# Two attentions and a gated MLP on one core: which PSUM banks the turn of maxima and the side products use, and the order in pair 22

## The chip, the cores and the metric

One core of a Trainium2 chip. The metric is the device time of one execution in microseconds. Before the change three timed runs gave 481.25, 480.57 and 481.23, median 481.23 us.

## What is computed

Two transformer blocks on x (2 x 512 x 128) with a context (2 x 154 x 96), all in 32-bit precision. Block 0 is a cross attention with 16 heads of 8 and an MLP. Block 1 is a self attention, a cross attention on the context (both with 16 heads of 64) and a gated MLP, each behind a layernorm. Cut to what matters here:

```python
def _attn(xq, xc, Wq, Wk, Wv, Wo, bo):
    q = (xq @ Wq).reshape(B, N, HEADS, D_HEAD)
    k = (xc @ Wk).reshape(B, S, HEADS, D_HEAD)
    v = (xc @ Wv).reshape(B, S, HEADS, D_HEAD)
    scores = jnp.einsum('bnhd,bshd->bhns', q, k) * scale
    attn = jax.nn.softmax(scores, axis=-1)
    out = jnp.einsum('bhns,bshd->bnhd', attn, v).reshape(B, N, HEADS * D_HEAD)
    return out @ Wo + bo
x = _attn(_ln(x, g1, b1), _ln(x, g1, b1), Wq1, Wk1, Wv1, Wo1, bo1) + x
x = _attn(_ln(x, g2, b2), context, Wq2, Wk2, Wv2, Wo2, bo2) + x
x = _geglu_ff(_ln(x, g3, b3), Wp, bp, Wf, bf) + x
```

## The kernel before

The program is written engine by engine with semaphores; nothing reorders it. The attentions of block 1 are a loop over 32 pairs `g` of heads (two heads of 64 fill 128 partitions): pairs 0 to 15 are the self attention (batch 0, then 1), pairs 16 to 31 the cross attention. A pair's softmax is computed with keys on partitions, so the maxima over keys, one for each query, are needed as a row that is added to the scores in the accumulation.

For pair `g` TensorE does, in `attention` (L925):

- `all_scores(g)` (L874): the scores in chunks of keys (four in a self pair, two in a cross pair). A chunk is three products of rounded and rest parts (L714) and the product that adds the row of maxima (L717). Between them lie the products for the maxima of pair `g + 1`, with queries on partitions (`head_max`, L680).
- `side_before(g)`, then `project(g + 2)` (queries and keys of a later pair; L625, in a cross pair also L669).
- `turn_pair(g + 1)` (L694): four transposes that turn the maxima of the next pair, of 128 queries each, into the row.
- `side_behind(g)`, `denominators` (L749) and `weigh(g, c)` (L734), the product of the exponentials with the values, into PV.

The side steps are other parts of the network that are laid into the loop: values (`VALUES`), the spread of the inverse denominators over the partitions (`spread_inverse`, L776, by the table `SPREADS`), output projections (L787), and the turns of the layernormed features (`turn`, L503). In pair 21 the turn of the second batch's features for the cross attention comes last of all; pair 22 projects with them for pair 24, and pair 30 has the turn for the last layernorm.

PSUM has 8 banks. Four are two bank pairs `ST0` and `ST1`, the ring of scores; two, `M0` and `M1`, serve the maxima; the last two are PV and DEN. `claim` hands out the ring's pairs in turn and waits until the use two claims back is freed; `claim_m` does the same with the single banks M0 and M1:

```python
def claim(key, freed, count):
    k = len(s_uses)
    if k >= 2:
        pe.wait_ge(*s_uses[k - 2])
    s_uses.append((freed, count))
    ring[key] = k % 2
    return ST[k % 2]
```

Chunks of scores (freed by the exponential), projections (freed by VectorE's rest part, `lo`), values, the turn of the maxima (freed by ScalarE's copy of the row, `mrow_set`) and some spreads use the ring. Each maxima product claims one bank M, which VectorE's reduction (L1645, in cross pairs L1647) frees.

ScalarE's order in a pair: the copy of the weighted sum of the pair before out of PV (`weighted`, L1313), the exponentials (L1305), values, the rounded part of the projection (`leading`, L1286 or L1288 and L1289), the row of maxima (`maxima_rows`, L1295). In pair 22 the features come first of all (`scale_features(2, 1)`, L1264 full and L1266 rounded). VectorE's: the reductions of the maxima of pair g + 1, the rest part (`trailing`), and side steps: in pair 22 the rest of the features (`trailing_features`, L1619: full less rounded part). The projection of the first pair of a batch waits for it (`xl_done`). GpSimd sums exponentials (L1139, L1143), adds bias rows (L1102) and finishes layernorms.

## Time and profile before

| | |
|---|---|
| timed runs, median (3) | 481.23 us |
| the profiled execution | 483.17 us |
| its span, first to last instruction | 481.4 us |
| TensorE busy | 461.4 us, 96% |
| VectorE, ScalarE, GpSimd busy | 253.5, 255.9, 215.3 us |
| mean granted clock of TensorE | 0.996 |

The profiled execution takes 1.8 us more than its span, and 1.9 us more than the median of the timed runs. Busy time of TensorE is the union of its instructions; their ends are modelled and overlap with the next start, so that a short wait between two of them shows as a longer distance between starts, and not as idle time.

### The profile page before, as it was taken

To read this page: it belongs to the slowest core of one execution; us is meant where nothing else is said; L and a number is where in the kernel's file an instruction comes from. 1 tells how busy PE (TensorE), PEld (TensorE's weight loads), DVE (VectorE), ACT (ScalarE), POOL (GpSimd) and SP (SyncE) were. 2 spreads that over 40 slices of the span, in tenths; PEclk is the share of its full clock that TensorE was granted. 3 is DMA by queue.
4 is the path that set the end of the run, shared out by engine and by line. 5 is a ranking of instruction groups with operands and counts; after the bars stand their busy time and mean duration, and the time that the engine had idled before them with its cause. 6 is when DMAs were issued, how large, how long until landed. Compare 5 with 4: busy or idle time off the path is not lost.

```text
span 481.4 us, 7219 instructions
## 1 busy us (share of the span) xinstructions
PE 461.4 (96%) x2870; PEld 279.6 (58%) x2870; DVE 253.5 (53%) x485; ACT 255.9 (53%) x358; POOL 215.3 (45%) x188
## 2 busy tenths in 40 slices
PE   7999897999999999999999999999998999999896
PEld 4655553566555665654555855555575555664596
DVE  2766736565744473547645566236633446432763
ACT  3754564465557365655545446555515675437623
POOL 5576101036873775544445556744227233245010
PEclk9999999999999999999999999999999999999999
DMA  8400000000000100000001100020010000000001
GB/s 264 178 0 2 1 1 0 1 1 0 1 0 1 33 1 1 0 0 2 1 0 45 34 0 2 1 67 0 1 45 0 2 1 0 2 1 0 1 2 43
DMA packets 7984, 8.89 MB, mean 18 GB/s; under 512 B 560, under 2 KB 6128, under 8 KB 7952
## 3 DMA queue, kind: packets, MB, share of 16 engines
q1 hardware_dynamic: 7952, 8.44, 5.6%
q8 instruction: 23, 0.38, 0.3%
q14 instruction: 9, 0.07, 0.0%
HBM read 7.92 MB, written 0.52 MB: 18 GB/s over the span
## 4 chain that ended last, share of the span: by engine, by line
PE 86%; DVE 6%; ACT 5%; issue 2%; DMA 1%; SPq 0%; DVEq 0%
PE PV L734 17%; PE ST L714 14%; PE ST L625 10%; PE M L680 7%; PE ST L717 5%; PE M L787 4%; PE ST L694 3%; PE DEN L749 3%; ACT PT L1305 2%; PE ST L645 2%; PE M L829 1%; PE ST L350 1%; PE ST L383 1%; PE ST L669 1%; PE M L625 1%
## 5 line engine op out<-in xcount | busy, mean ns | idle before, releaser
L1139 POOL TENSOR_TENSOR psums<-PT 128x1024 f32<-128x1024 f32 (+1 forms) x32 | 76.6, 2393 | 148.7 <-ACT PT L1305 148.6
L1305 ACT ACTIVATE PT<-ST 128x1024 f32<-128x1024 f32 (+1 forms) x96 | 98.1, 1025 | 41.4 <-PE ST L717 38.1
L714 PE MATMUL ST<-R 64*128 64x512 f32 (+1 forms) x576 | 111.8, 405 | 0.2 <-ACT xh L1266 0.2
L1645 DVE TENSOR_REDUCE maxw<-M 128x1 f32<-128x512 f32 x128 | 82.4, 686 | 40.3 <-PE M L680 36.9
L734 PE MATMUL PV<-PT,V 128*64 128x512 f32 (+1 forms) x384 | 89.5, 601 | 0.0
L1143 POOL TENSOR_TENSOR psums<-psums,PT 128x1024 f32<-128x1024 f32 x32 | 76.0, 2375 | 2.5
L714 PEld LDWEIGHTS ST<-R 64*128 64x128 f32 (+1 forms) x576 | 64.5, 171 | 16.1 <-ACT PT L1305 5.9
L680 PE MATMUL M<-R 64*128 64x512 f32 (+1 forms) x256 | 68.1, 350 | 0.8 <-DVE AT L1672 0.6
L680 PEld LDWEIGHTS M<-R 64*128 64x128 f32 x256 | 38.6, 184 | 34.1 <-issue 21.0
L734 PEld LDWEIGHTS PV<-PT,V 128*64 128x64 f32 (+1 forms) x384 | 24.7, 136 | 53.4 <-issue 53.3
L1313 ACT ACTIVATE AT<-PV 128x512 f32<-128x512 f32 x32 | 19.2, 599 | 61.6 <-PE PV L734 61.6
L717 PE MATMUL ST<-mrows,onesr 64*128 64x512 f32 (+1 forms) x192 | 46.2, 392 | 0.0
L1647 DVE TENSOR_REDUCE maxw<-M 128x2 f32<-128x308 f32 x64 | 27.7, 475 | 34.3 <-PE M L680 34.2
L1633 DVE TENSOR_TENSOR R<-ST,R 128x1024 fp32r<-128x1024 f32 x16 | 19.6, 1224 | 45.7 <-ACT R L1286 45.7
L1102 POOL TENSOR_TENSOR X<-X,rows 128x128 f32<-128x128 f32 x24 | 10.4, 466 | 44.4 <-DVE xnT L1559 44.3
L717 PEld LDWEIGHTS ST<-mrows,onesr 64*128 64x128 f32 (+1 forms) x192 | 23.7, 171 | 2.5
L1635 DVE TENSOR_TENSOR R<-ST,R 128x512 fp32r<-128x512 f32 x16 | 11.1, 692 | 25.1 <-ACT R L1289 25.1
L787 PE MATMUL M<-Wo,AT 128*128 128x128 f32 x192 | 21.9, 275 | 0.0
L787 PEld LDWEIGHTS M<-Wo,AT 128*128 128x128 f32 x192 | 21.7, 192 | 0.0
L1286 ACT ACTIVATE R<-ST 128x1024 fp32r<-128x1024 f32 x16 | 16.4, 1026 | 9.8 <-PE ST L625 9.8
L1504 DVE TENSOR_REDUCE maxw<-ST 128x4 f32<-128x616 f32 x20 | 15.9, 801 | 10.8 <-PE ST L383 10.6
L694 PE MATMUL ST<-ident,maxw 128*128 128x128 f32 x128 | 20.2, 281 | 1.2 <-DVE AT L1530 0.6
(251 smaller groups left out, 688.4 us busy)
## 6 DMA issues: line engine op xcount, KB each, us to landing
Wo<-in_wo SPq DMA_DIRECT2D x2, 512.0 KB, 6.1
xnT<-in_xT SPq DMA_DIRECT2D x2, 256.0 KB, 3.6
psums<-in_sel SPq DMA_DIRECT2D x1, 512.0 KB, 4.8
X<-in_x SPq DMA_DIRECT2D x1, 512.0 KB, 6.1
w<-in_w SPq DMA_DIRECT2D x2, 256.0 KB, 6.3
PT<-in_wq SPq DMA_DIRECT2D x1, 512.0 KB, 6.8
PT<-in_wk SPq DMA_DIRECT2D x1, 512.0 KB, 7.3
PT<-in_wv SPq DMA_DIRECT2D x1, 512.0 KB, 7.4
```

Of the source, the lines that this page charges most:

```text
L625: ins = pe.matmul(dst, stationary[v], moving[w], start=(n == 0), stop=(n == 2))
L680: ins = pe.matmul(m[:, at:at + ph.NK], r[head(h), 0, qt * P:(qt + 1) * P], r[head(h), 1, 0:ph.NK], start=True, stop=True)
L694: ins = pe.transpose(u[:, 0, qt * P:(qt + 1) * P], maxw[:, g % 2, qt, :], ident[:, :])
L714: ins = pe.matmul(u[0:ph.KC, h, :], R[head(h), g % 3, part_k, 1, k], R[head(h), g % 3, part_q, 0, :], start=(n == 0), stop=False)
L717: ins = pe.matmul(u[0:ph.KC, h, :], onesr[head(h), 0:ph.KC], mrows[head(h), g % 2, :], start=False, stop=True)
L734: ins = pe.matmul(PV[head(h), :], V[0:ph.KC, b * ph.NC + c, (2 * j + h) * HD:(2 * j + h + 1) * HD], PT1[0:ph.KC, g % 2, c, h, :], start=(c ...
L787: ins = pe.matmul(u[:, t * P:(t + 1) * P], AT[:, j, (TB * b + t) * P:(TB * b + t + 1) * P], Wo[:, j, :], start=(j == 0), stop=(j == PAIRS ...
L1139: ins = pool.tensor_tensor(s, p[:, 0], p[:, 1], ALU.add)
L1143: ins = pool.tensor_tensor(s, s, p[:, c], ALU.add)
L1305: act.activation(PT1[0:ph.KC, g % 2, c], bank(("st", g, c))[0:ph.KC, :, :], ACT.Exp, scale=HD ** -0.5).then_inc(ph.exp, 1)
L1645: ins = dve.tensor_reduce(maxw[:, g % 2, c, HD * h:HD * h + 1], m[:, :], AX, ALU.max, negate=True)
L1647: ins = dve.tensor_reduce(maxw[:, g % 2, 2 * c:2 * c + 2, HD * h], m[:, 0:2 * S].rearrange("p (t k) -> p t k", t=2), AX, ALU.max, negate=True)
```

## The change

It has four parts. The turn of the maxima takes a bank M in place of a pair of the ring. The values of pairs 6 and 7 and the spreads behind the turn (pairs 9, 10, 11, 18, 19, 26, 27), which took both banks M one after the other, take a pair of the ring, and ScalarE or VectorE reads them with one instruction over two banks instead of two. In pair 22 ScalarE copies the weighted sum of pair 21 behind the two exponentials, not ahead of them. In pair 22 VectorE computes the rest of the features between the two units of maxima, not behind both.

```diff
-            def values(n, t, among_maxima=False):
+            def values(n, t):
...
-                if among_maxima:
-                    u = [claim_half(("v", n, t, v), va_done[n], t + 1, True) for v in range(2)]
-                else:
-                    both = claim(("v", n, t), va_done[n], t + 1)
-                    u = both[:, 0, :], both[:, 1, :]
+                u = claim(("v", n, t), va_done[n], t + 1)
...
             def turn_pair(g):
 
                 pe.wait_ge(m_free, m_count[0])
-                u = claim(("turn", g), mrow_set, g + 1)
+                u = claim_half(("turn", g), mrow_set, g + 1, True)
                 for qt in range(TB):
-                    ins = pe.transpose(u[:, 0, qt * P:(qt + 1) * P], maxw[:, g % 2, qt, :], ident[:, :])
+                    ins = pe.transpose(u[:, qt * P:(qt + 1) * P], maxw[:, g % 2, qt, :], ident[:, :])
                 ins.then_inc(t_full, 1)
...
-            def spread_inverse(k, m, among_maxima=False):
+            def spread_inverse(k, m):
 
                 pe.wait_ge(recw_done, k + 1)
-                done = 4 * k + m + 1
-                if among_maxima:
-                    u = [claim_half(("bc", k, m, v), norm_done, done, True) for v in range(2)]
-                else:
-                    both = claim(("bc", k, m), norm_done, done)
-                    u = both[:, 0, :], both[:, 1, :]
+                u = claim(("bc", k, m), norm_done, 4 * k + m + 1)
...
-                act.activation(mrows[:, g % 2, :], bank(("turn", g))[:, 0, :], ACT.Copy).then_inc(mrow_set, 1)
+                act.activation(mrows[:, g % 2, :], half_bank(("turn", g)), ACT.Copy).then_inc(mrow_set, 1)
...
-                    if g >= 1:
+                    if g >= 1 and g != 22:
                         weighted(g - 1)
                     if g == 2:
                         root(0, 1)
                     for c in range(ph.units):
                         exponentials(g, c)
+                    if g == 22:
+                        weighted(g - 1)
...
-                if among_maxima:
-                    for v in range(2):
-                        ins = dve.tensor_tensor(t[:, v], half_bank(("bc", k, m, v)), t[:, v], ALU.mult)
-                else:
-                    ins = dve.tensor_tensor(t, bank(("bc", k, m))[:, :, :], t, ALU.mult)
-                ins.then_inc(norm_done, 1)
+                dve.tensor_tensor(t, bank(("bc", k, m))[:, :, :], t, ALU.mult).then_inc(norm_done, 1)
...
                         for k in maxima_units(g + 1):
                             maxima(g + 1, k)
+                            if g == 22 and k == 0:
+                                trailing_features(2, 1)
                     if g in (18, 26):
                         inverse_split(g // 8 - 1)
-                    if g == 22:
-                        trailing_features(2, 1)
```

TensorE's order of work stays as it is; its banks and waits change. At the start of the attention, from the last values product to the second chunk of pair 0 (a wait's name is the semaphore: `mrow_set` is the row copy, `mul0_done` VectorE's normalising for block 0, `v1a_done` the copy of values), before:

```order
L625 MATMUL ST1<-Wv,xh 128x512
L694 MATMUL ST0<-ident,maxw 128x128 [waits mul0_done,m_free,consts_set]
L694 MATMUL ST0<-ident,maxw 128x128 x3
L680 MATMUL M1<-R 128x512 [waits m_free,self_hi,v1a_done]
L714 MATMUL ST1<-R 128x512 [waits self_lo]
L714 MATMUL ST1<-R 128x512
L680 MATMUL M0<-R 128x512 [waits m_free]
L714 MATMUL ST1<-R 128x512 x4
L717 MATMUL ST1<-mrows,onesr 128x512 [waits mrow_set]
L717 MATMUL ST1<-mrows,onesr 128x512
L714 MATMUL ST0<-R 128x512 [waits mrow_set]
```

and now:

```order
L625 MATMUL ST1<-Wv,xh 128x512
L690 MATMUL M1<-ident,maxw 128x128 [waits m_free,consts_set]
L690 MATMUL M1<-ident,maxw 128x128 x3
L676 MATMUL M0<-R 128x512 [waits m_free,self_hi,mul0_done]
L710 MATMUL ST0<-R 128x512 [waits self_lo]
L710 MATMUL ST0<-R 128x512
L676 MATMUL M1<-R 128x512 [waits mrow_set]
L710 MATMUL ST0<-R 128x512 x4
L713 MATMUL ST0<-mrows,onesr 128x512 [waits mrow_set]
L713 MATMUL ST0<-mrows,onesr 128x512
L710 MATMUL ST1<-R 128x512 [waits v1a_done]
```

The turn (L694, now L690) has gone from ST0 to M1 and waits for `m_free` alone of the two buffers' semaphores; the second of the maxima products waits for `mrow_set`; `mul0_done` is awaited at the first chunk.

TensorE from the turn in pair 19 to the first chunk of pair 20 (`recw` and `sel` are the spread's operands, `norm_done` VectorE's multiplication with it), before:

```order
L694 MATMUL ST0<-ident,maxw 128x128 [waits norm_done,m_free]
L694 MATMUL ST0<-ident,maxw 128x128 x3
L776 MATMUL M0<-recw,sel 128x512 [waits m_free,recw_done]
L776 MATMUL M1<-recw,sel 128x512
L734 MATMUL PV<-PT,V 64x512 [waits cross_pvs,cross_exp]
L734 MATMUL PV<-PT,V 64x512
L734 MATMUL PV<-PT,V 64x512 [waits cross_exp]
L734 MATMUL PV<-PT,V 64x512
L680 MATMUL M0<-R 128x154 [waits norm_done,cross_hi,cross_lo]
L680 MATMUL M0<-R 128x154
L714 MATMUL ST1<-R 77x512 [waits cross_lo]
L714 MATMUL ST1<-R 77x512
```

and now:

```order
L690 MATMUL M0<-ident,maxw 128x128 [waits m_free]
L690 MATMUL M0<-ident,maxw 128x128 x3
L767 MATMUL ST0<-recw,sel 128x512 [waits norm_done,recw_done]
L767 MATMUL ST0<-recw,sel 128x512
L730 MATMUL PV<-PT,V 64x512 [waits cross_pvs,cross_exp]
L730 MATMUL PV<-PT,V 64x512
L730 MATMUL PV<-PT,V 64x512 [waits cross_exp]
L730 MATMUL PV<-PT,V 64x512
L676 MATMUL M1<-R 128x154 [waits m_free,cross_hi,cross_lo]
L676 MATMUL M1<-R 128x154
L710 MATMUL ST1<-R 77x512 [waits cross_lo]
L710 MATMUL ST1<-R 77x512
```

The turn waits for `m_free` alone, the spread lies in the ring and waits for the spread before it, and the first maxima product waits for a reduction (`m_free`), not for `norm_done`.

ScalarE in pair 22, from the features to the row of maxima, before:

```order
L1264 ACTIVATE xnT<-ST0,cols 128x512 [waits t_done2]
L1266 ACTIVATE xh<-ST0,cols 128x512
L1313 ACTIVATE AT<-PV 128x512 [waits cross_pv]
L1305 ACTIVATE PT<-ST1 77x1024 [waits cross_sum,cross_pv,cross_st]
L1305 ACTIVATE PT<-ST0 77x1024 [waits cross_st]
L1288 ACTIVATE R<-ST1 128x512 [waits cross_proj]
L1289 ACTIVATE R<-ST1 128x154
L1295 ACTIVATE mrows<-ST0 128x512 [waits t_full]
```

and now:

```order
L1255 ACTIVATE xnT<-ST0,cols 128x512 [waits t_done2]
L1257 ACTIVATE xh<-ST0,cols 128x512
L1291 ACTIVATE PT<-ST1 77x1024 [waits cross_sum,cross_pv,cross_st]
L1291 ACTIVATE PT<-ST0 77x1024 [waits cross_st]
L1299 ACTIVATE AT<-PV 128x512 [waits cross_pv]
L1274 ACTIVATE R<-ST1 128x512 [waits cross_proj]
L1275 ACTIVATE R<-ST1 128x154
L1281 ACTIVATE mrows<-M0 128x512 [waits t_full]
```

The copy out of PV has moved from ahead of the exponentials to behind them. VectorE in the same pair, before:

```order
L1647 TENSOR_REDUCE maxw<-M1 128x2 [waits m_full]
L1647 TENSOR_REDUCE maxw<-M0 128x2 [waits m_full]
L1647 TENSOR_REDUCE maxw<-M1 128x2 [waits m_full]
L1647 TENSOR_REDUCE maxw<-M0 128x2 [waits m_full]
L1619 TENSOR_TENSOR xl<-xnT,xh 128x512 [waits xn_done2,xfull1_done]
L1635 TENSOR_TENSOR R<-ST1,R 128x512 [waits cross_hi]
```

and now:

```order
L1635 TENSOR_REDUCE maxw<-M0 128x2 [waits m_full]
L1635 TENSOR_REDUCE maxw<-M1 128x2 [waits m_full]
L1607 TENSOR_TENSOR xl<-xnT,xh 128x512 [waits xn_done2,xfull1_done]
L1635 TENSOR_REDUCE maxw<-M0 128x2 [waits m_full]
L1635 TENSOR_REDUCE maxw<-M1 128x2 [waits m_full]
L1623 TENSOR_TENSOR R<-ST1,R 128x512 [waits cross_hi]
```

The rest of the features stands between the two units of reductions.

## Rows read from the trace of the kernel before

**Rows 1.** The page, part 4: shares of the chain by engine.

```profile
PE 86%; DVE 6%; ACT 5%; issue 2%; DMA 1%; SPq 0%; DVEq 0%
```

**Rows 2.** Timeline, pairs 16 and 19: start us, us, engine line op out<-in xcount [idle before <-releaser].

```profile
317.47 2.15 ACT L1305 ACTIVATE PT<-ST 77x1024 f32<-77x1024 f32 x2 [0.70 <-PE ST L717]
...
318.55 0.73 PE L625 MATMUL ST<-xh,Wv 128*128 128x512 f32 x2
...
319.34 0.43 PE L669 MATMUL ST<-ctxT,w 96*128 96x154 f32 x2
...
319.76 0.63 PE L694 MATMUL ST<-ident,maxw 128*128 128x128 f32 x4
...
321.31 1.94 PE L734 MATMUL PV<-PT,V 77*64 77x512 f32 x8
...
323.18 0.34 PE L680 MATMUL M<-R 64*128 64x154 f32 x1
...
341.35 0.42 PE L669 MATMUL ST<-ctxT,w 96*128 96x154 f32 x2
...
341.63 0.63 PE L694 MATMUL ST<-ident,maxw 128*128 128x128 f32 x4
```

**Rows 3.** Timeline, TensorE from pair 19 to pair 20.

```profile
342.65 1.94 PE L734 MATMUL PV<-PT,V 77*64 77x512 f32 x8
...
344.88 0.31 PE L680 MATMUL M<-R 64*128 64x154 f32 x1 [0.30 <-DVE AT L1672]
```

**Rows 4.** Timeline, pair 22 and the first row of pair 23.

```profile
367.62 0.77 ACT L1266 ACTIVATE xh<-ST,cols 128x512 fp32r<-128x512 f32 x1
...
368.76 2.08 ACT L1305 ACTIVATE PT<-ST 77x1024 f32<-77x1024 f32 x2
...
369.38 0.40 PE L717 MATMUL ST<-mrows,onesr 64*77 64x512 f32 x2
...
370.12 0.68 DVE L1619 TENSOR_TENSOR xl<-xnT,xh 128x512 fp32r<-128x512 f32 x1
...
371.06 1.08 PE L625 MATMUL ST<-xh,Wv 128*128 128x512 f32 x2 [1.28 <-ACT PT L1305]
...
377.07 0.34 PE L680 MATMUL M<-R 64*128 64x154 f32 x1
```

**Rows 5.** Stretch behind the wait: PE, PEld, DVE, ACT, POOL busy (x), PEclk, DMA, GB/s.

```profile
371.20:374.60 3.40, 3.40 (x13) 2.23 (x17) 0.66 (x2) 1.39 (x3) 2.07 (x1) 0.50 0.00 0
```

**Rows 6.** Timeline, end of pair 30.

```profile
435.58 0.86 DVE L1647 TENSOR_REDUCE maxw<-M 128x2 f32<-128x308 f32 x2 [0.71 <-PE M L680]
...
436.10 0.63 PE L503 MATMUL ST<-ident,xnT 128*128 128x128 f32 x4
...
437.23 0.63 PE L694 MATMUL ST<-ident,maxw 128*128 128x128 f32 x4 [0.49 <-ACT PT L1305]
```

**Rows 7.** Timeline, the start of the attention.

```profile
98.53 1.02 ACT L1277 ACTIVATE V<-ST 128x1024 f32<-128x1024 f32 x1 [1.86 <-PE ST L625]
...
99.09 0.63 PE L694 MATMUL ST<-ident,maxw 128*128 128x128 f32 x4 [0.60 <-DVE AT L1530]
...
99.76 0.60 ACT L1295 ACTIVATE mrows<-ST 128x512 fp32r<-128x512 f32 x1 [0.20 <-PE ST L694]
...
100.00 0.39 PE L680 MATMUL M<-R 64*128 64x512 f32 x1
```

**Rows 8.** Timeline, row copy behind pair 17 and the second maxima of pair 19.

```profile
327.60 0.60 ACT L1295 ACTIVATE mrows<-ST 128x512 fp32r<-128x512 f32 x1
...
329.60 0.34 PE L680 MATMUL M<-R 64*128 64x154 f32 x2
```

**Rows 9.** Timeline, two subtractions' neighbours: POOL in pair 21, POOL and DVE in pair 30.

```profile
366.68 1.72 POOL L1102 TENSOR_TENSOR X<-X,rows 128x128 f32<-128x128 f32 x4
...
437.16 2.37 POOL L1139 TENSOR_TENSOR psums<-PT 77x1024 f32<-77x1024 f32 x1 [1.48 <-ACT PT L1305]
...
438.51 1.57 DVE L1619 TENSOR_TENSOR xl<-xnT,xh 128x512 fp32r<-128x512 f32 x1 [2.07 <-ACT xh L1266]
```

More of the change, by code:

```diff
@@ L642, in values @@
                     if n == 0:
-                        ins = three(u[v], (xh[:, k], xl[:, k]), (Wv[:, 0, c], Wv[:, 1, c]))
+                        ins = three(u[:, v, :], (xh[:, k], xl[:, k]), (Wv[:, 0, c], Wv[:, 1, c]))
                     else:
-                        ins = pe.matmul(u[v][0:r], ctxT[:, k], Wv2[:, c], start=True, stop=True)
+                        ins = pe.matmul(u[0:r, v, :], ctxT[:, k], Wv2[:, c], start=True, stop=True)
                 ins.then_inc(v_done[n], 1)
@@ L764, in last_denominators @@
                 ins.then_inc(cross_att.den, 1)
-            def spread_inverse(k, m, among_maxima=False):
+            def spread_inverse(k, m):
                 pe.wait_ge(recw_done, k + 1)
-                done = 4 * k + m + 1
-                if among_maxima:
-                    u = [claim_half(("bc", k, m, v), norm_done, done, True) for v in range(2)]
-                else:
-                    both = claim(("bc", k, m), norm_done, done)
-                    u = both[:, 0, :], both[:, 1, :]
+                u = claim(("bc", k, m), norm_done, 4 * k + m + 1)
                 for v in range(2):
-                    ins = pe.matmul(u[v], sel[:, 2 * m + v, :], recw[:, :], start=True, stop=True)
+                    ins = pe.matmul(u[:, v, :], sel[:, 2 * m + v, :], recw[:, :], start=True, stop=True)
                 ins.then_inc(spread_done, 1)
@@ L914, in side_behind @@
                 if g in (6, 7):
-                    values(0, VALUES[g][1] + 1, True)
+                    values(0, VALUES[g][1] + 1)
                 if g in SPREADS and SPREADS[g][1] is not None:
-                    spread_inverse(g // 8 - 1, SPREADS[g][1], True)
+                    spread_inverse(g // 8 - 1, SPREADS[g][1])
                 if g in (12, 20):
@@ L1267, in scale_features, with values @@
                                scale=cols[:, g:g + 1], bias=cols[:, c:c + 1]).then_inc(xn_done[n], 1)
-            def values(n, t, among_maxima=False):
+            def values(n, t):
                 r = P if n == 0 else SC
                 act.wait_ge(v_done[n], t + 1)
-                if among_maxima:
-                    for v in range(2):
-                        ins = act.activation(V[0:r, t, N * v:N * (v + 1)], half_bank(("v", n, t, v))[0:r], ACT.Copy)
-                else:
-                    ins = act.activation(V[0:r, t, :].rearrange("p (u n) -> p u n", u=2), bank(("v", n, t))[0:r], ACT.Copy)
-                ins.then_inc(va_done[n], 1)
+                act.activation(V[0:r, t, :].rearrange("p (u n) -> p u n", u=2), bank(("v", n, t))[0:r], ACT.Copy).then_inc(va_done[n], 1)
             def leading(g):
@@ L1360, in attention @@
                     if g in (6, 7):
-                        values(0, VALUES[g][1] + 1, True)
+                        values(0, VALUES[g][1] + 1)
                     if g in (8, 16, 24):
@@ L1662, in inverse_split, with normalise @@
                                          ALU.mult, ALU.add).then_inc(recw_done, 1)
-            def normalise(k, m, among_maxima=False):
+            def normalise(k, m):
                 ph, b = (self_att, cross_att)[k // B], k % B
@@ L1669, in normalise @@
                 t = AT[:, 2 * m:2 * m + 2, b * N:(b + 1) * N]
-                if among_maxima:
-                    for v in range(2):
-                        ins = dve.tensor_tensor(t[:, v], half_bank(("bc", k, m, v)), t[:, v], ALU.mult)
-                else:
-                    ins = dve.tensor_tensor(t, bank(("bc", k, m))[:, :, :], t, ALU.mult)
-                ins.then_inc(norm_done, 1)
+                dve.tensor_tensor(t, bank(("bc", k, m))[:, :, :], t, ALU.mult).then_inc(norm_done, 1)
             def residual(n, b):
@@ L1712, in attention @@
                     if g in SPREADS and SPREADS[g][1] is not None:
-                        normalise(g // 8 - 1, SPREADS[g][1], True)
+                        normalise(g // 8 - 1, SPREADS[g][1])
                     if g == 1:
```

## The prediction

> **What bounds the kernel.** I read the chain first: 86% of the span is TensorE's [rows 1], and its busy share is 96%. So the kernel is a queue of TensorE instructions, and the change is worth what it takes out of the waits in that queue. Then the waits of TensorE, and then, because the records of matmuls overlap and so cover short waits, the timeline: the distance from one start to the next, at a place that waits and at one that doesn't. Last the granted clock by stretches. A pair below is a pass of the main loop, numbered by g from 0 to 31; pairs from 16 are the cross attention.
>
> Four places wait on what the change touches. (1) In a cross pair the turn of maxima (L694) takes a bank pair of the ring of scores, and so waits for the exponential of the chunk two claims back. In pair 16 the exponentials run from 317.47 to 319.62, and the turn starts 0.42 us behind the last projection (319.34 to 319.76); in pair 19, where that wait is over, 0.28 us (341.35 to 341.63) [rows 2]. (2) The spread of the inverse in pair 19 holds both banks of the maxima until VectorE has multiplied, and the first maxima of the next pair start 2.23 us behind the weighing (342.65 to 344.88) [rows 3] where 1.87 us is the distance without a wait (321.31 to 323.18) [rows 2]. (3) In pair 22 the projection waits until 371.06 with 1.28 us of idle time before it [rows 4], and right behind this the granted clock is 0.50, that is 1.2 GHz, from 371.2 to 374.6 [rows 5]. (4) The last turn starts 1.13 us behind the turn of the layernorm (436.10 to 437.23) [rows 6].
>
> **The change part by part.**
>
> *The turn goes to a bank of the maxima.* It no longer waits for an exponential, only for the maxima that it reads anyway. Of the cross pairs six (16, 17, 21, 23, 25, 29) show the distance 0.42 us: 6 x (0.42 - 0.28) = 0.84. Two more (14, 24) show 0.47: 2 x 0.19 = 0.38. The turns behind pairs 18 and 26 wait as well, but I count nothing: the spread behind them waits for the inverse. Together **1.22 us**. In the other self pairs the six matmuls of the projection cover the last exponential; nothing there. What is late next: no exponential is awaited before the second chunk's weighing, more than 1 us on, and the rounding of the projection by ScalarE starts as before.
>
> *The last turn*, behind pair 30: its maxima are reduced at 436.44 (435.58 and 0.86), and with 0.14 us to wake TensorE it starts at 436.58 in place of 437.23 [rows 6]: **0.65 us**. The tail behind it hangs on ScalarE, which is fed by the last scores, so it moves with them.
>
> *The spreads go to the ring.* The maxima of pairs 21 and 29 (computed during pairs 20 and 28) find their bank free, and the wait moves to the second chunk of scores, over 1 us later, when VectorE is done. 2.23 - 1.87 = 0.36, at two places: **0.72 us**. That VectorE and ScalarE now take two banks in one instruction, not two, is off the path; nothing. The same for the values moved in pairs 6 and 7: their ring claim needs the copy of the values before, which is over by then, and the next user of the bank comes a whole weighing later.
>
> *Pair 22.* Before, the low part of the features ran behind both units of maxima, 370.12 to 370.80, and the projection started at 371.06, 0.26 us later [rows 4]. (The row names the exponential, which ended at 370.84; but that is the one of the chunk just before, and the projection claims the bank pair of the chunk before that.) Now VectorE does it between the units. ScalarE has the high part ready at 368.39 (367.62 and 0.77). With 0.14 to wake VectorE (as TensorE needed behind the exponential, 319.62 to 319.76 [rows 2]) and 0.68 for the subtraction it ends at 369.21, and the projection could start at 369.47. The matmuls in front of it are issued by 369.38 [rows 4], and three of 512 columns take 0.79 us (318.55 to 319.34 [rows 2]), so one more distance of some 0.25 us brings it to 369.63: 1.43 us less idle time. The other thing it waits for, the first exponential, started at 368.76 behind the copy of the weighted sum; now that copy is not in front of it, and it runs from about 368.4 to 369.4. The copy comes behind both exponentials, from 370.84 on (368.76 and 2.08), takes 0.60 like the copy of the same size at 99.76 [rows 7], and is over at 371.44, ahead of the weighing at about 372.2 (the turn at 370.7 and the 1.55 from 319.76 to 321.31 [rows 2]). From the projection to the next pair's first maxima the same work takes 4.63 us in pair 16 (318.55 to 323.18) [rows 2], 4.49 without the turn's wait, but 6.01 here (371.06 to 377.07) [rows 4]: 1.52 us is the half clock. I take it that the clock stays at 2.4 GHz when the idle time before it is gone, and count 1.43 + 1.52 = **2.95 us**. Of the half clock's share the bounds are 0 and 1.52.
>
> *What it costs.* The turn's bank is now free only when ScalarE has copied the row of maxima, and the second maxima taken in the next pair need that bank. Behind pair 17 the copy ends at 328.20 and those maxima come at 329.60 [rows 8]: 1.40 us of room, nothing. The one place without a weighing in between is the start. There the copy of the last values ends at 99.55; the row copy, 0.60 us, can follow at once and ends at 100.15, and the second maxima, now at 100.00 [rows 7], move to about 100.2: **0.2 us** lost. Bounds: a gain of 0.7, by which the turn itself comes earlier (its wait for VectorE, 0.60 us of idle time at 99.09, goes), and a loss of 0.4. I take the value near the loss since the row names what ends last.
>
> The sum: 1.22 + 0.65 + 0.72 + 2.95 - 0.20 = 5.34 us. It is made against the profiled execution, 483.17 us, and would bring it to 477.8. The median of the timed runs is 481.23, 1.94 us below that; all terms but the half clock are waits that every execution has, so I take the difference over: 481.23 - 5.34 = **475.9 us**.
>
> **The rivals.**
>
> *The half clock is not won back* (0.20). For it speaks that other waits with idle time, 0.60 and 0.49 us [rows 7, 6], did not bring the clock down, so that nothing shows which size does; that the wait of the second chunk for the layernorm's turn stays; and that no timed run shows its clock. Against it: the only row at 0.50 in the steady part stands right behind the longest wait of TensorE. Then 5.34 - 1.52 = 3.82 is gained: 477.4 us. The Trainium skill has a rule on this side (TensorE: Matmul & The Clock Gate, "A second HAM failure mode: psum-queue depth-cycling"): many short idles between groups of matmuls, as banks of PSUM change hands, can be enough for the clock to swing between its two levels. By that rule the chunked waits that stay could take the clock down too; this trace has them in all 31 pairs and one fall (the mean granted clock is 0.996, which is 3.4 us at one half).
>
> *The low part is slowed by GpSimd* (0.07). The same subtraction took 1.57 us at 438.51, while GpSimd added from 437.16 on, and 0.68 at 370.12, with GpSimd idle. The bias rows on GpSimd run until 368.40 [rows 9], 0.1 us before the new place of the subtraction. If they overlap, it ends up to 1.57 - 0.68 = 0.89 us later, 0.16 of which is slack (369.47 to 369.63): 0.73 less gain, 476.6 us. The skill's GPSIMD Engine Reference, section Specifications, says why: GpSimd shares VectorE's SBUF interface when VectorE reads two SBUF inputs; the two rows agree.
>
> *The cross pairs' gain is taken by the next wait* (0.07). Every term is 0.14 to 0.19 us, and the projection of the next pair still waits for its first exponential. That wait hangs on TensorE's own scores, so I expect it to move along. If not, 1.22 is lost: 477.1 us.
>
> *The banks of the maxima become the bound* (slower, 0.02). Between the turn and the row copy VectorE has one bank instead of two. Should the copy end behind the second maxima in the middle of the loop, each of 31 pairs loses the difference; from 1.40 us of extra delay of ScalarE on it begins, and at 0.2 us a pair it is 6.2 us: 481.23 - 5.34 + 6.2 = 482.1 us. The rows give no reason for such a delay.
>
> *The change moves nothing* (0.02): if the turn in fact waited for the maxima, and pair 22 for an exponential, the time stays at 481.2. The ends of the waits speak against it [rows 2, 4].
>
> **How the numbers follow.** The forecast holds 0.62. A difference of 0.2%, about 1 us, is what a measurement of this kernel can tell. All cases but the last two are faster by more than that: 0.96 faster, 0.02 within, 0.02 slower. The range: the forecast's own bounds are 0.5 us at the start on either side and errors of single waits; the upper end takes in the half clock kept with part of another loss, 477.4 + 1.0 = 478.4. Below, the start may gain its 0.7 in place of losing 0.2, and the rest may be short waits that the overlapping records hide: 1.2 us, 474.7.
>
> **What would show it.** Turns 0.28 us behind the projection in all cross pairs; no row of the clock at 0.50 between 366 and 375; the projection of pair 22 about 2.0 us behind the start of the high part on ScalarE (before 3.4), with the low part between the reductions; the last turn 0.5 us behind the one before; the next maxima 1.87 us behind the weighing in pairs 20 and 28; at the start the second maxima waiting for the row copy. I am wrong if the clock falls at another place, if TensorE waits for the row copy in the loop, or if the span falls by less than 3.5 us.

## The result, and the profile after

The changed kernel takes 476.96 us, median of 4 runs (476.05 to 477.88), where the kernel before took 481.14 (4 runs): ratio 0.9906, 95% interval 0.9876 to 0.9935. That is 4.2 us less, where 5.3 was forecast. Timed again in the experiments, it took 477.29 (6 runs) beside 481.6 (11 runs): 0.9924, interval 0.9897 to 0.995. The mean granted clock of the changed kernel was 1.00 in all four of its executions.

The profiled executions differ by more, 6.66 us (483.17 and 476.51). The page of the changed kernel, its head, part 1 and the shares of part 4:

```profile
span 474.6 us, 7208 instructions
PE 457.7 (96%) x2870; PEld 279.2 (59%) x2870; DVE 253.4 (53%) x478; ACT 255.2 (54%) x356; POOL 216.0 (46%) x188
PE 88%; DVE 5%; ACT 5%; issue 2%; DMA 1%; SPq 0%; DVEq 0%
```

The kernel is still a queue of TensorE instructions: the same 96%, 3.7 us less of it busy (the half clock and the short waits that the modelled ends hid), and 88% of the chain in place of 86% [rows 1].

Ahead of everything that the change touches lies the loading, and it differs from execution to execution. The first projection of the self attention, timeline of the kernel before, then of the changed one:

```profile
84.28 0.70 PE L625 MATMUL ST<-xh,Wq 128*128 128x512 f32 x2 [0.84 <-DVE xl L1619]
```

```profile
83.03 0.70 PE L625 MATMUL ST<-xh,Wq 128*128 128x512 f32 x2 [0.83 <-DVE xl L1607]
```

From this start to the end of the span, the **body** below, it is 481.4 - 84.28 = 397.1 us before and 474.6 - 83.03 = 391.6 after. Of the 6.8 us between the spans 1.25 are loading, 1.57 the half clock (next section), and some 3.9 the change.

The places, on the timeline of the changed kernel (as in [rows 2]: start, us, engine, line, op, out<-in, count, idle time and its releaser). Lines have moved: the turn is L690, first maxima L676, scores L710 and L713, spread L767, weighing L730, exponential L1291, row copy L1281. Pairs 16 and 19:

```profile
316.18 2.13 ACT L1291 ACTIVATE PT<-ST 77x1024 f32<-77x1024 f32 x2 [0.71 <-PE ST L713]
...
318.05 0.43 PE L665 MATMUL ST<-ctxT,w 96*128 96x154 f32 x2
...
318.32 0.60 PE L690 MATMUL M<-ident,maxw 128*128 128x128 f32 x4
...
340.00 0.60 PE L690 MATMUL M<-ident,maxw 128*128 128x128 f32 x4
...
340.36 0.71 PE L767 MATMUL ST<-recw,sel 128*128 128x512 f32 x2
...
341.00 1.94 PE L730 MATMUL PV<-PT,V 77*64 77x512 f32 x8
...
342.87 0.34 PE L676 MATMUL M<-R 64*128 64x154 f32 x1
```

The turn of pair 16 starts 0.27 us behind the projection (318.05 to 318.32) where it was 0.42 [rows 2], and no longer waits for the exponentials to end at 318.31; the two times only happen to fall together. The maxima taken in pair 20 start 1.87 us behind the weighing (341.00 to 342.87), where it was 2.23 [rows 3]. Pair 22 and the first maxima of pair 23:

```profile
364.68 1.70 POOL L1093 TENSOR_TENSOR X<-X,rows 128x128 f32<-128x128 f32 x4
...
365.42 0.77 ACT L1257 ACTIVATE xh<-ST,cols 128x512 fp32r<-128x512 f32 x1
...
366.08 1.01 ACT L1291 ACTIVATE PT<-ST 77x1024 f32<-77x1024 f32 x1
...
366.29 0.69 DVE L1607 TENSOR_TENSOR xl<-xnT,xh 128x512 fp32r<-128x512 f32 x1 [0.31 <-ACT xh L1257]
...
367.52 0.73 PE L625 MATMUL ST<-xh,Wv 128*128 128x512 f32 x2
...
371.98 0.34 PE L676 MATMUL M<-R 64*128 64x154 f32 x1
```

The subtraction ends at 366.98, the projection starts at 367.52 with no idle time in its row: 2.10 us behind the start of the high part, 3.44 before [rows 4]. From there to the next maxima it is 4.46 us, in place of 6.01. The window of the changed kernel that answers to [rows 5] has the full clock:

```profile
368.00:371.00 3.00, 3.00 (x21) 1.36 (x21) 0.93 (x3) 2.29 (x5) 2.27 (x1) 1.00 0.03 5
```

The end of pair 30, where the last turn comes 0.46 us behind the turn of the layernorm and not 1.13 [rows 6]:

```profile
430.05 0.63 PE L503 MATMUL ST<-ident,xnT 128*128 128x128 f32 x4
...
430.51 0.60 PE L690 MATMUL M<-ident,maxw 128*128 128x128 f32 x4
```

And the start of the attention, against [rows 7]:

```profile
97.10 0.62 PE L690 MATMUL M<-ident,maxw 128*128 128x128 f32 x4
97.30 1.02 ACT L1264 ACTIVATE V<-ST 128x1024 f32<-128x1024 f32 x1 [1.86 <-PE ST L625]
...
97.77 0.50 PE L676 MATMUL M<-R 64*128 64x512 f32 x1
98.22 0.59 ACT L1281 ACTIVATE mrows<-M 128x512 fp32r<-128x512 f32 x1
...
98.86 0.49 PE L676 MATMUL M<-R 64*128 64x512 f32 x1 [0.37 <-ACT mrows L1281]
```

The turn waits for VectorE no more, but the second maxima wait for the row copy, which stands behind the copy of values: the loss that was foreseen. It is also TensorE's only wait for the row copy in the list of waits of the changed kernel:

```profile
PE M L676 <- ACT mrows L1281: 0.4, 1, 0.4
```

Every one of these steps has moved as predicted, yet the sum was not reached. What is open at this point is the half clock: whether every execution pays it, and whether the wait brings it.

### The profile page after: what moved, and what is told of

Its sections match the earlier page's. It is cut to its first block, busy times and chain, and to the rows that moved or that the text cites. A ratio compares the mean times of both kernels' runs of the same rounds, so it can differ in the third digit from the quotient of the medians.

```text
span 474.6 us, 7208 instructions
## 1 busy us (share of the span) xinstructions
PE 457.7 (96%) x2870; PEld 279.2 (59%) x2870; DVE 253.4 (53%) x478; ACT 255.2 (54%) x356; POOL 216.0 (46%) x188
## 3 DMA queue, kind: packets, MB, share of 16 engines
HBM read 7.92 MB, written 0.52 MB: 18 GB/s over the span
## 4 chain that ended last, share of the span: by engine, by line
PE 88%; DVE 5%; ACT 5%; issue 2%; DMA 1%; SPq 0%; DVEq 0%
PE PV L730 18%; PE ST L710 14%; PE ST L625 11%; PE M L676 7%; PE ST L713 5%; PE M L778 5%; PE DEN L745 3%; PE M L690 3%; ACT PT L1291 2%; PE ST L641 2%; PE M L820 2%; PE ST L383 1%; PE ST L350 1%; PE ST L665 1%; PE DEN L467 1%
## 5 line engine op out<-in xcount | busy, mean ns | idle before, releaser
L1291 ACT ACTIVATE PT<-ST 128x1024 f32<-128x1024 f32 (+1 forms) x96 | 98.1, 1025 | 42.0 <-PE ST L713 38.4
L710 PE MATMUL ST<-R 64*128 64x512 f32 (+1 forms) x576 | 112.6, 406 | 0.2 <-ACT xh L1257 0.2
L730 PE MATMUL PV<-PT,V 128*64 128x512 f32 (+1 forms) x384 | 89.5, 601 | 0.0
L710 PEld LDWEIGHTS ST<-R 64*128 64x128 f32 (+1 forms) x576 | 64.9, 171 | 15.9 <-ACT PT L1291 6.3
L676 PE MATMUL M<-R 64*128 64x512 f32 (+1 forms) x256 | 68.6, 352 | 0.6 <-ACT mrows L1281 0.4
L676 PEld LDWEIGHTS M<-R 64*128 64x128 f32 x256 | 38.8, 184 | 34.7 <-issue 24.4
L730 PEld LDWEIGHTS PV<-PT,V 128*64 128x64 f32 (+1 forms) x384 | 24.7, 136 | 53.1 <-issue 53.0
L713 PE MATMUL ST<-mrows,onesr 64*128 64x512 f32 (+1 forms) x192 | 46.6, 393 | 0.0
L713 PEld LDWEIGHTS ST<-mrows,onesr 64*128 64x128 f32 (+1 forms) x192 | 23.9, 171 | 2.5
L1623 DVE TENSOR_TENSOR R<-ST,R 128x512 fp32r<-128x512 f32 x16 | 11.1, 692 | 23.8 <-ACT R L1275 23.8
L778 PEld LDWEIGHTS M<-Wo,AT 128*128 128x128 f32 x192 | 21.7, 192 | 0.0
L690 PE MATMUL M<-ident,maxw 128*128 128x128 f32 x128 | 19.2, 272 | 0.0
```

Source lines behind the costliest of these rows:

```text
L676: ins = pe.matmul(m[:, at:at + ph.NK], r[head(h), 0, qt * P:(qt + 1) * P], r[head(h), 1, 0:ph.NK], start=True, stop=True)
L690: ins = pe.transpose(u[:, qt * P:(qt + 1) * P], maxw[:, g % 2, qt, :], ident[:, :])
L710: ins = pe.matmul(u[0:ph.KC, h, :], R[head(h), g % 3, part_k, 1, k], R[head(h), g % 3, part_q, 0, :], start=(n == 0), stop=False)
L713: ins = pe.matmul(u[0:ph.KC, h, :], onesr[head(h), 0:ph.KC], mrows[head(h), g % 2, :], start=False, stop=True)
L730: ins = pe.matmul(PV[head(h), :], V[0:ph.KC, b * ph.NC + c, (2 * j + h) * HD:(2 * j + h + 1) * HD], PT1[0:ph.KC, g % 2, c, h, :], start=(c ...
L778: ins = pe.matmul(u[:, t * P:(t + 1) * P], AT[:, j, (TB * b + t) * P:(TB * b + t + 1) * P], Wo[:, j, :], start=(j == 0), stop=(j == PAIRS ...
```

## The experiments

The measure in most of them is the distance between the starts of two turns on the timeline, which agrees to 0.06 us between executions wherever a kernel does the same there (to 0.04 in the pairs shown). Theory A is the prediction's: the wait of pair 22 brings the clock down, so the change wins it back in every run. Theory B: the half clock comes in some executions only.

| turn to turn, us | before | e0 | e1 | e2 | after |
|---|---|---|---|---|---|
| pair 0 to 1 | 7.62 | 7.60 | 7.60 | 8.57 | 8.56 |
| 16 to 17 | 7.82 | 7.82 | 7.82 | 7.68 | 7.68 |
| 19 to 20 | 8.62 | 8.62 | 8.62 | 8.75 | 8.75 |
| 20 to 21 | 7.92 | 7.93 | 7.92 | 7.54 | 7.54 |
| 22 to 23 | 9.06 | 8.28 | 7.17 | 8.25 | 6.94 |
| 23 to 24 | 7.89 | 7.10 | 7.12 | 6.96 | 6.96 |
| 30 to 31 | 6.13 | 6.12 | 6.13 | 5.45 | 5.45 |
| body | 397.1 | 395.5 | 394.5 | 392.8 | 391.6 |

A second measure is the mean granted clock, which is on record for every execution timed in the experiments. The traced execution before, with 3.4 us at half in 481, has 0.996; so 0.996 tells of one such stretch and 1.00 of none, though not where it lies. Sorted by it, number of executions and median time (1.00 stands for 0.999 as well, in three executions; kernels run once are left out):

| executions of | at 1.00 | us | at 0.996 | us |
|---|---|---|---|---|
| `e0` (the kernel before) | 9 | 481.1 | 3 | 483.5 |
| the kernel before, timed beside `e0` to `e3` | 23 | 481.0 | 8 | 483.5 |
| the kernel before, timed beside `f1`, `e6`, `e7` and `e8` | 10 | 481.5 | 1 | 481.8 |
| the kernel before, timed beside the rest | 0 | | 1 | 483.4 |
| `e1` | 6 | 479.8 | 6 | 482.8 |
| `e2` | 8 | 479.2 | 0 | |
| `e3` | 12 | 481.3 | 0 | |
| the changed kernel, first time | 4 | 477.0 | 0 | |
| `f1` (the changed kernel) | 5 | 477.0 | 1 | 480.4 |
| `e6` | 2 | 477.6 | 4 | 479.3 |

**The kernel before, again** (`e0_before_again`, no edit).

> The kernel before, once more, for the granted clock and the span of each of its executions. Theory A (every execution before has the half clock behind the wait of pair 22): the mean granted clock is 0.996 in each, and the time is within 0.2% of the median of before, 481.1 us. Theory B (the half clock came in the one profiled execution and not in the timed ones): some or all executions show 1.00, and those are about 1.5 us shorter than one with 0.996, so near 479.7 where the other is at 481.2.

481.09 us (12 runs), ratio 0.9999 (0.9976 to 1.0023). Its profiled execution, 481.24, has the same wait in pair 22 and full clock behind it (timeline, then windows, of `e0_before_again`):

```profile
370.72 0.70 PE L625 MATMUL ST<-xh,Wv 128*128 128x512 f32 x2 [1.28 <-ACT PT L1305]
```

```profile
372.00:376.00 4.00, 4.00 (x30) 1.56 (x30) 1.28 (x3) 1.82 (x4) 0.95 (x1) 1.00 0.00 0
```

Against the first profile of the same program two distances are shorter, 0.78 and 0.79 us (pairs 22 and 23), together 1.57: that is the whole half clock, and the body differs by little else. Of the twelve executions nine have a mean clock of 1.00 and three 0.996, where theory A wanted 0.996 in each. So B holds: the same wait, and no fall in most executions. The median of the kernel before is that of executions without a fall. What B also expected, that those at 1.00 lie near 479.7, did not come about: they are at 481.1 and the three others at 483.5. That is 2.4 us between the groups where the traced fall costs 1.6; the rest isn't explained.

**The order of pair 22 alone** (`e1_order`).

```diff
-                    if g >= 1:
+                    if g >= 1 and g != 22:
                         weighted(g - 1)
...
+                    if g == 22:
+                        weighted(g - 1)
...
                             maxima(g + 1, k)
+                            if g == 22 and k == 0:
+                                trailing_features(2, 1)
...
-                    if g == 22:
-                        trailing_features(2, 1)
```

> The kernel before with the order of pair 22 alone changed (the copy out of PV behind the exponentials, the rest of the features between the two units of maxima); banks as before. Theory A: minus 2.9 us against before (1.4 of idle time and 1.5 of half clock), no row of the clock under 1.00. Theory B: minus 1.4 us only, since the timed executions of before have no half clock to win back. If the banks were what shortens pair 22: no gain.

The traced execution took 479.01, and its pair is 1.11 us shorter than e0's (8.28 to 7.17); 1.43 was expected of the idle time. On its timeline the projection has no idle time left:

```profile
367.02 0.69 DVE L1621 TENSOR_TENSOR xl<-xnT,xh 128x512 fp32r<-128x512 f32 x1 [0.31 <-ACT xh L1266]
...
368.24 0.73 PE L625 MATMUL ST<-xh,Wv 128*128 128x512 f32 x2
368.35 1.02 ACT L1305 ACTIVATE PT<-ST 77x1024 f32<-77x1024 f32 x1 [0.52 <-PE ST L717]
...
369.51 0.63 PE L694 MATMUL ST<-ident,maxw 128*128 128x128 f32 x4
```

Its turn, still in the ring, starts 0.14 us behind the end of the second exponential (369.37): the order's last 0.2 us need the other bank too. The median of the timed runs doesn't show the gain: 481.47 (12 runs), ratio 0.9985 (0.996 to 1.0011). They fall into two groups, and the clock tells them apart: the six from 479.0 to 480.4 have 1.00, the six from 482.5 to 483.0 have 0.996. At 1.00 e1 is 1.3 us below e0 (means 479.8 and 481.1), near the 1.1 of the trace; the median hides it because half of e1's executions have a fall. So taking the wait of pair 22 away doesn't keep the clock up. Where the six fell was not caught in a trace of `e1`; `e4_features` below, with the same edit of VectorE, fell in the MLP.

**The banks alone** (`e2_banks`: the change with pair 22's two edits taken back).

> The banks of the change alone (turn of maxima to a bank of the maxima, values and spreads to the ring), the order of pair 22 as before. My sum gives minus 2.4 us: 1.22 at the turns of the cross pairs, 0.65 at the last turn, 0.72 behind the spreads, 0.2 lost at the start; the wait of pair 22 stays at 1.2 to 1.4 us and with it, by theory A, the half clock. A rival: the new waits for the row copy cost as much as the turn gains, and the difference is under 1 us.

479.2 us (8 runs), ratio 0.9941 (0.9918 to 0.9965). The body is 2.7 us shorter than e0's, 2.39 was the sum of these terms. The start loses 0.20 net: the first distance is 0.97 longer and the turn before it 0.77 earlier. The wait of pair 22 stands (1.27), at full clock, and none of the eight executions has 0.996.

**A filled wait** (`e3_fill`: TensorE claims the bank pair of pair 24's projection first and computes two products of 256 columns into it, overwritten later, ahead of the wait for the features).

```diff
+                    if g == 24:
+                        u = claim(("proj", g), ph.lo, i + 1)
+                        hold(2, u[:, 0, :])
                     pe.wait_ge(xn_done[1 if ph is self_att else 2], b + 1)
...
-                u = claim(("proj", g), ph.lo, i + 1)
+                if g != 24:
+                    u = claim(("proj", g), ph.lo, i + 1)
```

> The kernel before with two dummy products of TensorE (256 columns, 32-bit, about 0.43 us each) laid into the wait of pair 22, in the bank pair that the projection then overwrites; the results are not used. The wait itself stays. If the idle time is what brings the clock down: no row under 1.00, and 1.5 us less than before in executions that have the half clock before. If something else does (the exponentials' wait, the mix of work in the stretch): the clock still falls and the time is as before.

481.28 us (12 runs), ratio 0.9984 (0.9964 to 1.0005). The idle time is gone, the time isn't, as both theories have it once e0 shows the clock up without a filling. None of the twelve executions has 0.996, but neither has any of e2's eight, whose wait is not filled, so this doesn't show what the filling does to the clock. One thing it does tell (timeline of `e3_fill`):

```profile
370.81 1.10 PE L339 MATMUL ST<-work 128*128 128x256 f32 x4
371.01 0.68 DVE L1623 TENSOR_TENSOR xl<-xnT,xh 128x512 fp32r<-128x512 f32 x1
...
371.84 0.70 PE L625 MATMUL ST<-xh,Wv 128*128 128x512 f32 x2
```

The claim, which needs the exponential, is granted before the products start, at 370.81; the projection comes 0.15 us behind the subtraction. So here the projection waited for the low part and not for the bank.

**The features' edit alone and the copy's alone** (`e4_features`, `e5_copy`: the VectorE half and the ScalarE half of e1's diff).

> The kernel before with the rest of the features of pair 22 between the two units of maxima, and nothing else. Then the first exponential, which still starts behind the copy out of PV and ends at about 369.8 by the clock of the first trace, is what the projection waits for. Both edits together took 1.11 us from the pair's length between turns (8.28 to 7.17). If the exponential binds now: about 0.9 us, 0.2 less than together. If the copy has no part in it: 1.11 us.

> The kernel before with the copy out of PV behind the two exponentials of pair 22, and nothing else. The projection still waits for the rest of the features, so the pair keeps its 8.28 us between turns (9.06 with the half clock, if that falls in this execution). If the exponential is what it waits for, as the row of the trace names: up to 0.5 us less.

With the features' edit pairs 22 to 23 take 7.16 us, all of e1's gain; with the copy's edit 8.29, none. Timeline of `e4_features`, then of `e5_copy`:

```profile
369.42 2.08 ACT L1305 ACTIVATE PT<-ST 77x1024 f32<-77x1024 f32 x2
...
370.58 0.70 PE L625 MATMUL ST<-xh,Wv 128*128 128x512 f32 x2
...
371.64 0.63 PE L694 MATMUL ST<-ident,maxw 128*128 128x128 f32 x4
```

```profile
366.54 1.01 ACT L1305 ACTIVATE PT<-ST 77x1024 f32<-77x1024 f32 x1
...
368.39 0.68 DVE L1621 TENSOR_TENSOR xl<-xnT,xh 128x512 fp32r<-128x512 f32 x1
...
369.33 0.71 PE L625 MATMUL ST<-xh,Wv 128*128 128x512 f32 x2 [1.28 <-ACT PT L1305]
```

In `e5_copy` the first exponential is over at 367.55, early, and the wait is as it was: the projection comes 0.26 us behind the subtraction (369.07). The exponential that the row names is the second one (368.08 to 369.10 there). That the projection doesn't need it is seen in `e4_features`, where the projection starts at 370.58 and the second exponential runs until 371.50: in e5 its end, 0.2 us before the start, is a coincidence.

The copy's move is worth nothing in the ring, but not because nothing waits for it. In `e4_features`, without that move, the first exponential ends at about 370.44 and the projection starts 0.14 us behind it. That is 0.54 us behind the start of the last products of the scores (370.04); in the changed kernel this distance is 0.33 (367.19 to 367.52). The 0.21 us don't show between the turns, since the turn, still in the ring, waits for the second exponential (371.50, start 371.64), as in e1. Once the turn has left the ring, the copy's move should be worth some 0.2 us: an estimate from these rows, since no run has the banks and the features' edit without the copy's.

`e4_features` took 482.75 in its one run. Its clock fell in the MLP behind the attentions, a place that no edit touches, behind waits of 1.08 and 0.42 us that every execution here has at L809 or L818 (windows of `e4_features`):

```profile
454.10:457.40 3.30, 3.30 (x18) 3.30 (x17) 2.56 (x3) 0.00 (x0) 0.00 (x0) 0.50 0.02 5
```

From the last turn to the end it is 45.74 us there and 44.16 in e0: 1.58 more. `e5_copy` took 479.87 in one run, at a body of 395.7 beside e0's 395.5: it had 1.5 us less of loading.

**The changed kernel again, and the row copy first** (`f1_after_again`; `e6_row_first`: the changed kernel with ScalarE's first row copy ahead of the last copy of values).

```diff
-                for t in range(TB):
+                for t in range(TB - 1):
                     values(0, t)
                 maxima_rows(0)
+                values(0, TB - 1)
```

> The changed kernel once more, for its time over more executions. Traces so far: an execution before without the half clock and the changed one differ by 3.9 us behind the load phase, and the load phase itself moves by up to 2.4 us from one execution to the next. Theory A (the half clock belongs to every execution before) would give 5.3 us less than before; theory B (it comes in some executions before) gives 3.9 to 4.4 us less in the medians.

> The changed kernel with ScalarE's row copy of pair 0 ahead of its copy of the last values. In the changed trace the second maxima product waits at 98.86 for the row copy (98.22 to 98.81), which waited for the values' copy (97.30 to 98.33). If that chain is the loss at the start, the product comes 0.3 to 0.5 us earlier and everything behind it moves by about as much: 0.3 us less from there on in the trace, too little for the timed median to show. If VectorE's reductions or the second chunk's bank (freed by the values' copy, now later) are the next limit: no gain, or a loss of up to 0.3.

f1's body is 391.6, as after; 477.29 us, 4.3 less than the 481.6 beside it, as B has it. In e6 the second maxima start 0.64 us behind the first (98.87 and 99.51), not 1.09 (timeline of `e6_row_first`):

```profile
98.20 0.62 PE L690 MATMUL M<-ident,maxw 128*128 128x128 f32 x4
98.86 0.60 ACT L1281 ACTIVATE mrows<-M 128x512 fp32r<-128x512 f32 x1 [2.32 <-PE M L690]
...
99.51 0.50 PE L676 MATMUL M<-R 64*128 64x512 f32 x1
```

The first distance is 8.13 in place of 8.56 and the body 391.2, 0.4 less: the trace has what was expected. The median of the timed runs doesn't: 479.12, ratio 0.9942 (0.9923 to 0.9961). Again the clock tells why: the four from 479.0 to 479.4 have 0.996, and the two at 1.00 (477.11, the traced one, and 478.02) lie among f1's five at 1.00 (476.6 to 477.9). The gain of 0.4 is thus seen in a trace alone. Why four of six executions had a fall here, and one of six in f1, and where it lay, is open.

**A longer wait** (`e7_longer_wait`: in the kernel before VectorE subtracts pair 22's low part three times over, with the same result).

> The kernel before with the subtraction of pair 22 computed three times, so that TensorE's wait there grows from 1.28 to about 2.7 us. If idle time makes the clock fall, more of it makes it more certain: a row at 0.50 behind the wait, and the pair 1.4 us longer by the wait and 1.5 us by the clock. If the fall before was unrelated to the wait: no row under 1.00, and 1.4 us more.

486.56 us in one run. The wait came to 4.76 us, not 2.7, since the last subtraction ran beside GpSimd (timeline of `e7_longer_wait`):

```profile
370.05 1.41 DVE L1706 TENSOR_TENSOR xl<-xnT,xh 128x512 fp32r<-128x512 f32 x2
...
370.85 2.81 POOL L1139 TENSOR_TENSOR psums<-PT 77x1024 f32<-77x1024 f32 x1 [2.52 <-ACT PT L1305]
...
371.49 2.71 DVE L1619 TENSOR_TENSOR xl<-xnT,xh 128x512 fp32r<-128x512 f32 x1
...
374.46 0.77 PE L625 MATMUL ST<-xh,Wv 128*128 128x512 f32 x1 [4.76 <-DVE xl L1619]
```

Its windows show the clock down within the wait and for 3.44 us of work behind it:

```profile
371.10:374.46 3.36, 0.00 (x0) 0.03 (x1) 3.07 (x2) 0.00 (x0) 2.55 (x1) 0.50 0.00 0
374.46:377.90 3.44, 3.44 (x13) 2.49 (x17) 0.45 (x1) 1.20 (x3) 0.00 (x0) 0.50 0.02 5
```

The body is 5.2 us longer than e0's, 3.5 by the wait (4.76 for 1.28) and the rest, 1.7, by the clock. So a wait of TensorE can bring the clock down, and this part of A stands. Behind the wait of 1.28 us the clock fell in one trace only; that this wait was the cause there is argued from the place and not shown.

**The turn alone in a bank of the maxima, and the side products alone in the ring** (`e8_turn_only`: turn_pair's edit and the row copy's in the kernel before; `e9_sides_only`: `e2_banks` without those two).

> The kernel before with only the turn (and its copy) moved to a bank of the maxima; values and spreads behind the turn keep both banks of the maxima. I expect the second product of each of these nine side steps to wait for the row copy: 0.6 us at two values, 1.15 at pairs 9 to 11, 0.7 to 0.8 at pairs 18, 19, 26, 27, together 7.7 us lost, against 1.9 won at the turns and 0.2 lost at the start: 6.0 us slower than before. A rival: the side steps' waits lie beside nothing that matters and the gain of 1.7 us stays.

> Values and spreads behind the turn in the ring, the turn still in the ring too, order of pair 22 as before. A side step behind the turn then claims the bank pair of the projection and waits for VectorE's rest part of it, which comes behind all reductions: about 2.1 us at each of the five places in the self pairs, 1.4 to 1.6 at the four in the cross pairs, 16 us in all, less 0.7 behind the spreads: about 15 us slower. A rival: the rest part is there by then and the 0.7 us is won alone.

Both are much slower than before: 493.24 and 503.16 us, one run each, bodies 11.1 and 21.7 us longer than e0's, where 6.0 and 15 were expected. The turn alone is awaited by the side products in M0 and M1, which claim both banks before the first product, so they need the whole row copy: 1.5 us at each of five places in the self attention, 1.2 and 0.9 (each twice) in the cross pairs. Of the 11.1, 1.6 is a half clock in the MLP. The sides alone sit in the ring behind the turn and the projection, and wait for VectorE's rest part (list of waits of TensorE, and a row of the timeline, of `e9_sides_only`):

```profile
PE ST L767 <- DVE R L1619: 6.0, 3, 2.0
PE ST L767 <- DVE R L1622: 5.5, 4, 1.4
PE ST L625 <- DVE R L1619: 4.6, 3, 2.0
```

```profile
187.68 1.22 DVE L1619 TENSOR_TENSOR R<-ST,R 128x1024 fp32r<-128x1024 f32 x1 [3.43 <-ACT R L1272]
...
189.05 0.47 PE L625 MATMUL ST<-Wv,xh 128*128 128x512 f32 x1 [1.98 <-DVE R L1619]
```

The list's 16.1 us and three half clocks behind waits of this size (the first at 190.0 to 193.4) make most of the 21.7. In the change neither wait exists: the turn has left the ring before the sides come, so that a side's two claims back is the scores' last chunk.

**The kernel before, a third time** (`g0_before_third`, no edit).

> The kernel before once more, for a third trace of the same program. Theory B: with the half clock about 1.6 us more between the turns of pairs 22 and 24 than without it (16.95 or 15.38 us), and which of the two comes is not set by the program; theory A was 16.95 in each. Everything between the load phase and pair 22 as in the other traces within 0.1 us.

481.95 us, wait of 1.29, clock at full, body 395.7, and 15.38 us between the turns of pairs 22 and 24. With `before`, `e0`, `e2`, `e5`, `e8` and `e9` that makes seven traces with the wait of 1.27 to 1.29 us in pair 22, of which one has the fall. The waits of the MLP, in all 14 traces, had a fall behind them in two (`e4` and `e8`).

## Why the prediction was right, and where not

The forecast case came in as to direction and for the waits of the banks and of pair 22; 476.96 lies inside the range, 1.1 us above the number. One term of the sum, the half clock, was not there to be won.

- **The turn in a bank of the maxima, 1.22 us, and the spreads, 0.72**: right at the places named (0.27 us and 1.87 us). In e2 against e0 the turns behind the eight pairs named come 0.14 to 0.24 us nearer to the one before, but for pair 24 with 0.06: 1.2 in all. The turns behind pairs 18 and 26, counted at nothing since "the spread behind them waits for the inverse", gained 0.18 each, of which the next distance gave 0.13 back.
- **The last turn, 0.65**: 0.67 measured (6.12 to 5.45).
- **The start, -0.20**: -0.20. The banks together gave 2.7 us where these four terms made 2.39; the difference is in distances of 0.02 to 0.18 us that I had not counted (behind pairs 18, 26, 20 and 28 the most).
- **Pair 22's idle time, 1.43**: 1.31 measured (e2 to after, both with banks), 1.11 without them. The prediction named both the low part and the first exponential, behind the copy, as what the projection needs. e4 and e5 show that the low part alone sets the 1.11; the other 0.2 comes with the turn out of the ring, and by e4's rows the copy's move has its part there, which no run shows by itself.
- **The half clock, 1.52**: it measures 1.57 where it occurs, but the step that failed is "all terms but the half clock are waits that every execution has, so I take the difference over", with "I take it that the clock stays at 2.4 GHz when the idle time before it is gone". I then took 1.52 off the median too. Of the timed executions of the kernel before in the table, 13 of 55 had a fall, so the median held none to win back; e0's and g0's traces, 481.24 and 481.95, show the same wait without it. Nor is the clock safe in the rest of the kernel when this idle time is gone: e1 has a fall in six of twelve, e6 in four of six and f1 in one of six, which is one in ten for the changed kernel with its first four.
- **The forecast without that term**: the sum is 3.82 and the forecast 477.4, which is the first rival's number, 0.4 us from the result; the rival reached it by the clock falling after the change as before it, which it did in none of the three traces of this order with these banks and in one of the changed kernel's ten timed executions. One in ten against 13 in 55 is too few to tell whether the change makes falls rarer. By the prediction's own sign (wrong "if the clock falls at another place") that one may count against it; its place was not traced. That the number came this close is in part luck: 0.3 us more than counted at the banks made up for a part of the 1.52. The 1.94 us between the profiled time and the median was a hint that I read and did not use: against e0 it was the half clock, 1.57, and 0.34 of loading.
- **GpSimd's rival**: it did not happen, because the bias rows end at 366.38, 0.09 us into the subtraction, which took 0.69. e7 shows its price beside a long GpSimd instruction: 2.71 us in place of 0.68. It ended 0.54 us behind the end of that instruction (373.66 to 374.20), and the slow one of [rows 9] 0.55 behind its neighbour's (439.53 to 440.08), as if most of the subtraction ran only then. The Trainium skill's rule on the shared SBUF interface (GPSIMD Engine Reference, section Specifications) agrees.
- **The banks as the bound** did not come about in the change. e8 shows that this side was less remote than 0.02 says: without the other half of the change it costs 9.5 us beside the half clock.
- **The next wait takes the cross pairs' gain, and nothing moves at all**: neither happened; in e2 the distances between turns shrank by what the waits had cost.
- **The Trainium skill's rule of many short idles** (TensorE: Matmul & The Clock Gate, "A second HAM failure mode: psum-queue depth-cycling"): no trace of the 14 has a fall behind the chunked waits alone; each of the seven followed a longer wait, of at least 1.08 us. For the falls in the other timed executions this isn't shown, as none of those was traced.

## What to carry to other kernels

When a profiled execution is slower than the median of the runs, ask first what it has that they don't: a term seen in one profile alone, a half clock above all, comes off the median only as often as it occurs there, and a second profile of the same program, and the mean granted clock of each timed run, are the cheapest experiments. Where the runs of a kernel fall into two groups, sort them by the clock before taking a median: e1's gain of 1.3 us is plain at 1.00 and lost in the median. Read a wait by what ends nearest before it in each queue it names, since the releaser in the row can be a bystander. An edit that is worth nothing alone may still count once another has removed the wait that hid it, as is estimated here for the copy's move in pair 22. In a ring of two banks count uses, not banks: one user moved alone makes another's "two claims back" a younger one, and two edits that gain 2.7 us together may cost 11 and 22 apart (one run each, half clocks included).

## What the runs showed that I had not expected

- The loading phase isn't steady: the first projection of the self attention starts at 82.43 (`e5_copy`) to 85.14 us (`e3_fill`), with the same code before it. Spans are better compared from there.
- The granted clock falls in some executions and not in others of the same program at the same wait: behind 1.27 to 1.29 us in one of seven traces, behind 1.98 to 2.02 us at three of five places in `e9_sides_only`. A traced fall costs 1.6 us (1.57 in `before`, 1.58 in `e4_features`), at 3.4 us of half clock. The timed executions with a fall are 2.4 us above those without in `e0` and 3.0 in `e1`; what makes up the difference is open.
- A VectorE subtraction of 128x512 reading two SBUF operands took 0.68 us alone, 1.57 [rows 9] and 2.71 beside additions of GpSimd.
